# Where two expert-weight splits stand in a joined attention and routing stage of a vision tower (Trainium2, one core)

## What is computed

```python
h = _L0_tok_ref(x, ...)                       # 4 images x 3136 tokens x 192
h = h + _L0_attn_ref(_layernorm(h), ...)      # gated linear attention, causal
h = h + _L0_ffn_ref(_layernorm(h), ...)       # mixture of 8 experts, 2 per token
h = h + _L1_attn_ref(_layernorm(h), ...)
h = h + _L1_ffn_ref(_layernorm(h), ...)

def _L0_ffn_ref(x, w1, b1, w2, b2, down_w, down_b, up_w, gamma, beta):
    logits = _gelu(x @ w1 + b1) @ w2 + b2
    routing = softmax(logits)
    topv, topi = top_k(routing, 2)
    ...
    z = _gelu(einsum('bsh,ehd->bsed', x, down_w) + down_b)
    expert_out = einsum('bsed,edh->bseh', z, up_w)
    ...
```

## Time and profile before

| What | Value |
|---|---|
| Median of 3 runs | 2765.31 us (2760.18 to 2765.52) |
| The profiled execution | 2763.42 us |
| Its span | 2761.6 us |
| Granted TensorE clock, mean | 0.889 of 2.4 GHz |
| Busy share of the span | PE 83%, DVE 72%, ACT 56%, POOL 36% |
| Joined stage, first GpSimd op to the barrier's release | 855.0 to 1453.0 us |
| Its 28 full passes | 878.0 to about 1396 us |
| Passes 28 to 30 with the zero fill | about 1396 to 1447 us |

### The profile page before, as it was taken

The page is one execution under the profiler, slowest core; times in us unless marked ns, Lnnn a source line. Parts: engine busy times, 40 slices in busy tenths (PEclk is TensorE's granted clock), DMA queues, the critical chain, the costliest instruction groups (busy, mean ns, idle before and its releaser), DMA issues. The chain is left out here.

```text
span 2761.6 us, 45420 instructions
## 1 busy us (share of the span) xinstructions
PE 2304.1 (83%) x14046; PEld 1669.4 (60%) x14047; DVE 1995.4 (72%) x5437; ACT 1551.1 (56%) x2693; POOL 1001.9 (36%) x1024
## 2 busy tenths in 40 slices
PE   8999999999996899999947999926778785666665
PEld 4444444444444888888836999925677674444443
DVE  6777777777764899999944444447697877889986
ACT  2444444444444688888734665626565651777776
POOL 1100100100000356565652444478776720344343
PEclk9999999999997999999967999967687896767777
DMA  2000000000002011111136777721111100000000
GB/s 57 0 18 13 0 18 13 0 9 1 0 1 89 13 49 53 50 52 50 55 113 202 254 255 256 251 74 51 48 44 42 47 12 22 21 23 23 26 26 26
DMA packets 69143, 162.81 MB, mean 59 GB/s; under 512 B 12977, under 2 KB 32342, under 8 KB 68702
## 3 DMA queue, kind: packets, MB, share of 16 engines
q1 hardware_dynamic: 39426, 94.27, 10.3%
q0 software_dynamic: 21504, 44.99, 5.7%
q10 hardware_dynamic: 8064, 21.68, 2.6%
HBM read 63.98 MB, written 63.88 MB: 46 GB/s over the span
## 5 line engine op out<-in xcount | busy, mean ns | idle before, releaser
L211 ACT ACTIVATE prob<-pscore 128x896 f32<-128x896 f32 x336 | 308.0, 917 | 422.3 <-PE pscore L293 422.3
L418 DVE TENSOR_REDUCE pmax<-ppre 112x1 f32<-112x512 f32 x656 | 424.4, 686 | 160.9 <-PE ppre L260 160.9
L307 PE MATMUL pout<-prob,xkey 128*64 128x448 f32 x1344 | 327.5, 566 | 0.4 <-ACT prob L211 0.4
L260 PE MATMUL ppre<-xh,yh 49*112 49x512 f32 x656 | 290.7, 445 | 7.8 <-DVE pmax L418 4.1
L723 POOL DMA_INDIRECT rows_in<-xr,idx x224 | 237.8, 1062 | 132.3 <-DVE idx L1245 73.8
L193 POOL CAST yh<-ynext 113x448 fp32r<-113x448 f32 x28 | 17.2, 614 | 666.1 <-DVE pmax L418 638.1
L260 PEld LDWEIGHTS ppre<-xh,yh 49*112 49x112 f32 x656 | 112.5, 172 | 239.0 <-issue 104.2
L1704 POOL DMA_INDIRECT yg<-rows_out,place x224 | 231.7, 1035 | 62.4 <-issue 62.1
L293 PE MATMUL pscore<-yh,xh 49*128 49x448 f32 x700 | 240.5, 421 | 0.4 <-DVE yh L438 0.4
L2219 POOL TENSOR_TENSOR yg<-y,gout 112x512 f32<-112x512 f32 x112 | 141.0, 1269 | 260.1 <-DVE y L2452 260.1
L1554 POOL TENSOR_TENSOR zl<-z,zh 128x448 fp32r<-128x448 f32 x126 | 144.3, 1145 | 219.7 <-ACT zh L1520 210.3
(11 more groups left out here) (388 smaller groups left out, 6580.4 us busy)
## 6 DMA issues: line engine op xcount, KB each, us to landing
wd<-down SPq DMA_DIRECT2D x63, 512.0 KB, 3.0
xb<-rows_in SPq DMA_DIRECT2D x63, 448.0 KB, 3.5
rows_out<-yb ACTq DMA_DIRECT2D x63, 336.0 KB, 3.2
out<-ho SPq DMA_DIRECT2D x28, 336.0 KB, 2.8
rows_in<-zero SPq DMA_DIRECT2D x15, 448.0 KB
rows_in<-xr,idx POOLq DMA_INDIRECT x224
yg<-rows_out,place POOLq DMA_INDIRECT x224
xkey<-in_xkey SPq DMA_DIRECT2D x4, 800.0 KB, 6.6
```

Source lines behind the costliest of these rows:

```text
L211: nc.scalar.activation(prob[j % 3][:, :, :], pscore[j % 2][:, :, 0:CH], ACT.Exp).then_inc(exped, 1)
L260: pe.matmul(out[:, :], yh1[rows, q * T:(q + 1) * T], xh[b % 2][rows, block * 512:(block + 1) * 512], start=True, stop=True, tile_position= ...
L307: mm = pe.matmul(pout[i * LO:(i + 1) * LO, 0:CH], xkey[b % 2][:, 2 * j + i, :], prob[j % 3][:, i, :], start=(j == 0), stop=(i == 1 and j = ...
L418: nc.vector.reduce_max(pmax[:, q, 2 * block + half:2 * block + half + 1], bank(u, depth), AX.X).then_inc(pre_max, 1)
```

## The change

It moves the two casts, the two subtractions and the memset from passes 0 to 2 of the joined stage to its passes 28 to 30, and reorders three calls of TensorE in passes 28 and 29.

- ScalarE: `high(0)` and `high(1)` stand in pass 28, behind `take_r(26)` and ahead of `take_hidden(26)`.
- VectorE: `split_low(0)` stands in pass 28 and `split_low(1)` in pass 29, behind `places` and ahead of `softmax_head`.
- GpSimd: the memset stands in pass 30, behind `scatter(26)` and ahead of `scatter(27)`; it no longer waits for `rstd_out`.
- TensorE: in pass 28 `wo_out(27, (2, 3))` stands ahead of `transpose_r(26)`; in pass 29 `rank(26)` stands ahead of `transpose_r(27)`. All other passes keep their order.

```diff
@@ gpsimd
-                if g == 2:
+                if g == NC + 2:
                     pool.wait_ge(R["high"], 2)
-                    pool.wait_ge(R["rstd_out"], 2)
                     nc.gpsimd.memset(down[64:128, :, 3, :].bitcast(F32), 0.0).then_inc(R["cleared"], 1)
                     pool.wait_ge(R["cleared"], 1)
@@ tensor
                 if here(g):
                     weights(g)
+                elif here(g - 1):
+                    wo_out(g - 1, (2, 3))
+                if not here(g - 1) and here(g - 3):
+                    rank(g - 3)
                 if here(g - 2):
                     transpose_r(g - 2)
-                if here(g - 1):
+                if here(g) and here(g - 1):
                     wo_out(g - 1, (2, 3))
...
-                if here(g - 3):
+                if here(g - 1) and here(g - 3):
                     rank(g - 3)
@@ scalar
                 if here(g - 2):
                     take_r(g - 2)
+                if g == NC:
+                    high(0)
+                    high(1)
...
                     normalise_route(g - 1, (2, 3))
-                if g < 2:
-                    high(g)
@@ vector
                     elu_out(g + 1)
+                if g >= NC and g - NC < 2:
+                    split_low(g - NC)
                 if here(g - 2):
                     softmax_head(g - 2)
...
                     share(g - 3)
-                if g < 2:
-                    split_low(g)
```

## The result

The changed kernel takes 2755.06 us (median of 20 runs, 2748.86 to 2764.65) against 2763.38 us for the kernel before (20 runs, 2756.37 to 2772.16). The ratio is 0.9971, with a 95% interval of 0.9962 to 0.9981. The forecast was 2755.4, against a median of three runs of 2765.31; the difference of the medians is 8.3 us (by the interval 5.3 to 10.5) where 9.9 was forecast. The head of the stage gained nearly what was predicted, the tail lost 1.1 us that was not, and the reason for the loss is something that the prediction had wrong: what ends the stage.

What follows compares the result with a forecast made beforehand. Bound: TensorE's waits for `h` in passes 1 and 2 and the half clock behind them. 1.90 + 2.8 + 2.96 + 2.2 = 9.9 us, tail +0.5 and -0.5 cancelling; 2765.31 - 9.9 = 2755.4 us, range 2750.5 to 2761.

Steps and rivals of the forecast that it cites:

- Contention, not first use: Pass 1: VectorE's subtraction slows GpSimd's factor; the rival, first use after idling, gave 2760.2 us, chance 0.07.
- The clock comes back: Passes 1 and 2 regain full clock; the rival, half-clock stretches stay, gave gain 4.86, 2760.5 us, chance 0.12.
- The clock term of pass 1: Pass 1, TensorE's work behind its wait for `h`: full clock gains 2.67 to 3.26 us, taken as 2.8.
- Pass 1's wait: Pass 1: TensorE's wait for `h` shrinks from 2.40 to 0.50 us, gaining 1.90.
- look like pass 3: The other 25 full passes: said to resemble pass 3 (17.83 us) and not be touched.
- The last rival: Passes 28 and 29: scatters lock out VectorE's moved subtractions; 7 us slower, 2772 us, chance 0.04.
- I take about 4: Tail: the moved subtractions hold GpSimd's scatters by about 4 us in all, bounds nothing and 4.55.
- The stage ends with the zero fill ... That leaves 5 us.: Stage end: the zero fill, landed at 1447.05, ends it; the last scatter, near 1442, has 5 us of room.
- the barrier waits for GpSimd: Stage end: one of the signs named in advance that would show the prediction wrong.
- The third rival: Tail: 6.35 us of delay makes GpSimd's last scatter land behind the fill; gain 7.8, 2757.5 us, chance 0.15.
- +0.5 for the fill: Tail: late scatters sharing DMA engines with the zero fill cost 0.5 us (0 to 1).
- -0.5 for TensorE's order: Pass 29: earlier ranks of chunk 26 gain 0.5 us; at most 1.56 gain or 1.2 loss.

Runs made afterwards that it cites:

- second_back: Changed kernel with the second cast and second subtraction put back in pass 1; median 2748.35 us, ratio 0.9996 to the kernel before.
- before_wait_moved: Kernel before, with only VectorE instead of GpSimd waiting for the scatters' landing; median 2754.17 us, ratio 0.9958.
- best: Changed kernel with the memset on VectorE behind its last count of rows, and VectorE waiting for the landing; 2750.90 us, ratio 0.9952 to the kernel before.
- memset_last: Changed kernel with the memset behind GpSimd's last scatter; median 2743.75 us, ratio 0.9982 to the kernel before.
- order_only: Kernel before with only TensorE's new order, splits and memset left where they were; median 2747.29 us, ratio 0.9995.
- late: Changed kernel, memset behind the last scatter, both subtractions only after the landing, GpSimd still waiting for it; 2759.15 us, ratio 0.9971 to the kernel before.
- late2: Changed kernel, memset behind the last scatter, both subtractions behind the memset, only VectorE waiting for the landing; 2752.38 us, ratio 0.9941 to the kernel before.
- late2_pad: late2 plus a 112x8 subtraction on VectorE at each place where the change has a long one; 2751.12 us, ratio 0.9952 to the kernel before.
- best2: best with the second subtraction also behind VectorE's last count, both started after GpSimd's last scatter is issued; 2746.70 us, ratio 0.9927 to the kernel before.
- doses: Changed kernel with one to five dummy copies of about 0.65 us ending VectorE's odd passes 5 to 25; one execution, 2778.59 us.

## Why the prediction was right, and where it was wrong

**Head, right.** 9.45 us against 9.9. *Contention, not first use*: the factor took 0.20 us as the first work of GpSimd after 37.18 us; that rival is out, and both passes gained. *The clock comes back*: 1.00 in passes 1 and 2, so that rival is out too. The clock term of pass 1 was 2.8 and measures 2.70 (8.02 less 5.32). *Pass 1's wait*: 1.90 forecast, 1.87 measured (2.40 less 0.53). Pass 2 gave 4.87 of 5.16; second_back, where it pays 5.93, shows that this term varies by a microsecond with the length of the half clock, and the 0.3 lie inside that. That all the other full passes "look like pass 3" was read from one of them: they took 18.1 to 19.1 us in that trace, not 17.8, but in both kernels, so the forecast did not suffer.

**Casts and subtractions in idle time, right.** `peak` waited 1.10 us for the logits behind the first subtraction (1.2 to spare had been forecast) and 4.89 behind the second. The last rival, VectorE locked out by scatters, did not come: the subtractions took 2.29 and 2.28 us beside them. It was the scatter that waited, each time. The rule of the Trainium skill ("SBUF — State Buffer", Who interferes with whom), that the two exclude each other for a whole instruction, agrees with these rows in that the two held scatters ended 0.87 and 0.82 us behind their subtraction, about a scatter's own length (0.94). It is not seen the other way round: the second subtraction began 0.04 us into a scatter that took its usual 0.94 us, and was not held.

**Size of the holds, wrong by a quarter.** "I take about 4": it was 2.04 and 0.96, 3.0 together, inside the bounds of 0 and 4.55. The second hold is short since its scatter was issued 1.20 us after the subtraction began. The step that failed there is taking both holds as whole ones. The last scatter was to end 3 us late, near 1442; it was 1.54 us late, the rest because GpSimd's second idle time, 1.43 us ahead of the scatters of chunk 26, was not counted.

**What ends the stage, wrong.** The step is "The stage ends with the zero fill ... That leaves 5 us." The rows for it were read for the end of the fill only; the end of the stage, 5.9 us later, was in front of me (the release at 1453.0 stands in the table ahead) and what lay between was not looked up. It is the last part of the 9.2 us of GpSimd's closing step. The prediction's own sign of being wrong, that "the barrier waits for GpSimd", is there. GpSimd ended the stage all the time, so its lateness counts from the first tenth, not "from 4.2 us of delay upward". The last scatter was 1.54 us later in relation to the last `weights`, the landing took up 0.4 of that, and 1.10 reached the barrier. The third rival, *GpSimd ends the stage*, had the right engine, by a sum with the wrong end in it; its gain of 7.8 us lies nearer to the measured 8.3 than the forecast's 9.9 does, though the interval of 5.3 to 10.5 holds both. That the forecast's time of 2755.4 was met all the same is partly luck: the median of three runs that it starts from lay 1.9 us above the median of twenty. What shows the true end is before_wait_moved: the fill unchanged, the landing 0.9 us later, the release 3.9 us earlier.

**Terms of the tail, wrong in size.** +0.5 for the fill and -0.5 for TensorE's order were to cancel; together they cost 1.1. The +0.5 stood for packets in the fill, and what it should have stood for is the lateness of GpSimd's closing step. The -0.5 rested on the router's idle time of 1.56 us, most of which was a stall of VectorE. Where the stall is, the new order brings `peak` 0.6 to 0.8 us forward; on the chip without it, it puts it back by 0.4 to 0.6. What each term is worth alone at the stage's end is not shown, since there is no profile of the kernel before that matches theirs in the length of its passes. That the sum of 0 came out within 1.1 us is luck.

## What to carry to other kernels

At a barrier, read the barrier's own line on every engine before saying what ends a stage: the last transfer to land may not be it, and an engine with a closing step of fixed length should reach that step as early as it can, with the waits for its transfers on an engine that closes quickly and has nothing left to do. A long two-input operation can be moved into VectorE's idle time, but a GpSimd operation that starts under it is held until it ends (0.96 to 2.04 us here), so ask whether GpSimd has idle time there too. A wait of TensorE of 2.1 to 3.0 us inside a pass cost from nothing to 3.0 us more in clock here, and one of 1.5 us or less nothing, so a small wait in the middle of a dense stretch can be worth more than its length. And compare a profile only with one from the same chip before reading tenths from it.

## What the runs showed of the hardware that was not expected

- GpSimd's closing step at the barrier took 9.205 to 9.208 us in every kernel where it came behind the landing wait or the memset, and where the wait was moved it ended 9.2 us behind GpSimd's last work (9.65 in before_wait_moved). It runs beside landing transfers. It was as long behind the 224 indirect DMAs of the later stage (8.59 us behind the last work) and 0.07 us at the barriers of stages that have none. Whether the number of indirect DMAs sets the length was not tried.
- The last packet of the scatters' queue came from 1.3 us (best, where much of the fill came later) to 5.3 us (memset_last) behind the end of the last scatter. It was 3.5 us in order_only and in the changed kernel, with the fill beside it as in memset_last, so the fill alone does not settle it.
- VectorE stood still for 4.8 to 5.5 us in late, late2 and late2_pad with its input there, and for 1 to 2.4 us at a time in best and best2. The trace names no releaser. Stalls of 0.9 to 1.8 us come in the kernel before, the changed one and every other kernel of the second and third chip, between 35 and 61 us behind the last `weights`, and none in the four kernels of the first chip. One small operation more in the place of the long one does not remove the long stall (late2_pad); its cause, and whether it is there when no profile is taken, is open.
- The program from the first to the last `weights` is the same in eleven kernels, but for one pass of second_back and the doses of doses. Without these two it took 476.7 and 478.1 us on the first chip and 488.5 to 495.7 in the other profiles. So most of the spread goes with the chip, and a profile pair says little about a part of a per cent: the pass and the distance from a fixed mark do.
